# Trainium2 kernel: the stage between two attentions with fp16 part products, its operands split by the attention before it

## The chip, the cores and the metric

One core of one Trainium2 chip. The metric is the device time of one execution in microseconds (us), as the median of several runs. Engines are named as in the profile: PE is TensorE (PEld its weight loads), DVE VectorE, ACT ScalarE, POOL GpSimd, SP SyncE; SPq and the like are their queues of instructions.

## The reference, cut to what matters

Two layers over 2 x 1024 tokens of 512 features. Each layer computes `x = x + s * g` from the normalized `x`, where `s` is an attention and `g` a gate. The end of the first layer and the start of the second, which the change is about:

```python
out = out.transpose(0, 2, 1, 3).reshape(B, S, LATENT)      # 16 heads x 64 = 1024 features
s = out @ w_o.T                                            # output projection, 1024 -> 512
x = x + s * g
xn = _layernorm(x, axis=-1)
q = (xn @ wq.T)                                            # 32 heads x 16
k = (xn @ wk.T); v = (xn @ wv.T)                           # 8 heads x 16
router_logits = jnp.einsum('bsd,hd->bsh', xn, Wr) + br     # gate: 8 experts
low = jnp.einsum('bsd,hrd->bshr', xn, A)                   # low-rank part, 8 x 16
```

The second attention picks chunks of keys by their largest score, so queries and keys are wanted at about fp32's precision.

## The kernel before, in words

The program is a row of phases, each a block in which every engine has its own list of instructions, ordered by hand, and waits on semaphores. Between two blocks the engines meet. The change touches `attend_phase` (first attention), `MiddleWeights` and `middle_phase` (stage between the attentions).

**`attend_phase`** (L1905) goes over 16 pairs of heads, `p` from 0 to 15 (4 groups of keys x 2 sequences x 2 pairs). A pair has 8 key tiles `kt` of 128 keys; with the causal mask tile `kt` has 1024 - 128 kt query columns, in one or two pieces of up to 512. A step `n` is 8 p + kt.
- TensorE (L1997 on) makes the scores of a piece as fp16 part products into one of four PSUM banks (L2012 to L2017), up to four pieces ahead of the step whose values it makes next. A bank is free when ScalarE has taken the piece four back. `values(n)` (L2028) multiplies the values with the exponentials in fp32 into `ps_o`; for tile 0 it waits until ScalarE has copied the former pair's `ps_o`. Behind tile 2, `sums(p - 1)` (L2039) adds up the former pair's exponentials over the keys into `ps_n`.
- ScalarE takes each piece's exponential (L2078) into a ring of four steps, `probs`; a step waits until TensorE and the adder of the step four back (VectorE for tiles 0 to 2, GpSimd for 3 to 7) are done. For slots of tile 3 and 4 it waits until GpSimd has added tile 4. Behind tile 0 it copies the former pair's output, `copy(p - 1)` (L2062).
- VectorE adds tiles 0 to 2 of both heads (`gather`, L2124 to L2129) and puts GpSimd's sum to them (`combine(p - 1)`, L2137). `divide(p - 1)` waits for TensorE's sums, takes the reciprocal of 128x1024 sums (L2145) and multiplies the output with it into `stage` (L2150).
- GpSimd adds tiles 3 to 7 (L2097 to L2102).
- SyncE's list loads the stage's weights at the start, the next group's queries, keys and values behind the end of a pair, and stores `stage` (L1964) of the former pair.

```python
            for p in range(ALL):
                gather(p, 0)
                gather(p, 1)
                if p > 0:
                    combine(p - 1)
                gather(p, 2)
                if p > 0:
                    divide(p - 1)
```

**`middle_phase`** (L2264) goes over four chunks `c` of 512 tokens. TensorE's list: `project(0)`, `project(1)`, then `rest(c)`, `project(c + 2)`, `gates(c)`.
- `project(c)` (L2388): for each of four tiles of 128 tokens eight fp32 products of 128x512; VectorE (`add`, L2533) multiplies with the gate and adds `x`. Two PSUM banks, so the third tile waits until VectorE has taken the first.
- VectorE's `norm(c)` (L2540 to L2548), with a power by GpSimd, gives `xn`.
- `rest(c)`: 16 transpositions (L2398), evicted by ScalarE into `xnT` (L2447); values, low-rank part and gate (L2406, 264 columns), evicted at L2451; queries and keys (L2412), five blocks of four fp32 products of 128x512, evicted at L2463. Then VectorE's softmax of the gate (`route`) and the rotation of queries and keys with their split into three bf16 parts (`rotate`, L2581 to L2593; GpSimd's share L2505, L2507).
- `gates(c)` (L2425): the gate's products, with ScalarE's silu.
VectorE's list per chunk is `add(c + 1)`, `route(c)`, `rotate(c)`, `norm(c + 1)`.

## Time and profile before

| what | us |
|---|---|
| median of 3 runs | 2363.93 (2362.97 to 2368.98) |
| the profiled execution: its time / its span | 2369.5 / 2367.7 |
| TensorE, VectorE, ScalarE, GpSimd busy, share of the span | 87%, 63%, 46%, 33% |
| first attention, first product to last multiply | 1051.5 to 1361.8 |
| wait until the stage between starts | 1361.8 to 1371.3 |
| stage between the attentions | 1371.3 to 1664.1 |
| mean granted clock of TensorE | 0.946 |

The table's stages are read from the timeline. Durations below come from this one execution; they can be set against its own time, and that stands 5.6 us above the median of the runs. In the timeline a row gathers neighbouring instructions of one line; a row's form is that of its longest, and the bracket tells how long the engine sat idle before it and what ended that.

### The profile page before, as it was taken

How to read it: one execution, taken by the hardware profiler on the slowest of the kernel's cores; microseconds unless marked ns; L12 is line 12 of the kernel's file. 1: busy time of each engine (PE TensorE's matmuls, PEld its weight loads, DVE VectorE, ACT ScalarE, POOL GpSimd, SP SyncE). 2: the span in 40 equal slices, each digit the busy share in tenths (PEclk: the TensorE clock that was granted, in tenths of full speed). 3: DMA queues.
4: the chain of work that ended last, by engine and by line, in shares of the span. 5: the costliest groups of instructions: out<-in, count | busy, mean ns of one | idle time of the engine just before them, and what ended most of it. 6: DMA issues, size and time to landing. Idle time of an engine off the chain costs nothing. (4 is left out here: it accounts for less than half of the span.)

```text
span 2367.7 us, 46673 instructions
## 1 busy us (share of the span) xinstructions
PE 2058.6 (87%) x19128; PEld 1009.8 (43%) x19128; DVE 1489.3 (63%) x2992; ACT 1100.8 (46%) x1987; POOL 771.9 (33%) x735
## 2 busy tenths in 40 slices
PE   7999989998647898979999789987588888888878
PEld 3444435555213333445555434443244444443434
DVE  3534354443559999716777725445888888888813
ACT  1212135555324333227777502324277777777760
POOL 0102212222447456504444402223343333433310
PEclk9999999999879899989999989997799999999999
DMA  6120101101412121362222264132936455364424
GB/s 240 36 89 36 67 19 32 32 14 44 140 43 83 54 67 32 107 208 75 90 82 76 76 175 143 58 79 76 216 59 84 69 72 81 58 89 65 59 79 142
DMA packets 149338, 198.03 MB, mean 84 GB/s; under 512 B 57154, under 2 KB 85956, under 8 KB 146564
## 3 DMA queue, kind: packets, MB, share of 16 engines
q1 hardware_dynamic: 147540, 181.41, 30.9%
q10 hardware_dynamic: 1584, 13.63, 1.6%
q8 instruction: 151, 2.47, 0.5%
q14 instruction: 63, 0.52, 0.1%
HBM read 134.69 MB, written 60.29 MB: 82 GB/s over the span
## 5 line engine op out<-in xcount | busy, mean ns | idle before, releaser
L3112 DVE TENSOR_REDUCE f_chunk_max<-f_ps_a 128x64 f32<-128x1024 f32 x320 | 319.7, 1033 | 47.4 <-PE f_ps_a L2856 25.0
L2985 ACT ACTIVATE conv_in<-f_ps_s 128x512 f32<-128x512 f32 x480 | 258.5, 602 | 86.6 <-PE f_ps_s L2887 42.7
L2856 PE MATMUL f_ps_a<-conv_in 128*32 128x512 bf16 (+3 forms) x3072 | 201.0, 340 | 42.1 <-DVE f_chunk_max L3112 25.4
L2078 ACT ACTIVATE d_probs<-d_ps_s,d_shift 128x512 f32<-128x512 f32 (+3 forms) x384 | 196.7, 584 | 82.7 <-PE d_ps_s L2017 72.8
L2887 PE MATMUL f_ps_s<-f_qs,f_ks 128*32 128x512 bf16 x2304 | 208.3, 382 | 23.3 <-ACT f_qs L2976 14.7
L1420 PE MATMUL c_ps_c<-conv_in,c_wT 128*128 128x512 f16 x768 | 186.2, 402 | 18.5 <-DVE c_odd L1721 14.1
L3052 POOL TENSOR_SCALAR f_absent<-f_rest 128x576 f32<-128x576 f32 x32 | 54.4, 1700 | 304.9 <-DVE f_rest L3129 180.7
L2909 PE MATMUL f_ps_o<-conv_in,f_v 128*32 128x512 f32 (+2 forms) x1152 | 125.9, 522 | 28.3 <-ACT conv_in L2985 27.4
L2976 ACT ACTIVATE f_qs<-f_ps_s 32x512 bf16<-32x512 f32 x192 | 112.8, 587 | 75.6 <-PE f_ps_s L2870 73.3
L2028 PE MATMUL d_ps_o<-d_probs,conv_in 128*64 128x512 f32 (+3 forms) x768 | 146.1, 488 | 0.0
L2856 PEld LDWEIGHTS f_ps_a<-conv_in 128*32 128x32 bf16 x3072 | 71.8, 98 | 164.3 <-DVE f_chunk_max L3112 68.6
L2388 PE MATMUL e_ps_s<-e_oT,conv_in 128*128 128x512 f32 x256 | 118.7, 626 | 23.2 <-DVEq L64 17.4
L2012 PE MATMUL d_ps_s<-conv_in 128*64 128x512 f16 (+3 forms) x768 | 126.4, 330 | 8.8 <-POOL d_ones L2086 8.8
L2145 DVE RECIPROCAL d_inverse<-d_ps_n 128x1024 f32<-128x1024 f32 x16 | 104.9, 6558 | 44.2 <-PE d_ps_n L2039 44.2
L1420 PEld LDWEIGHTS c_ps_c<-conv_in,c_wT 128*128 128x128 f16 x768 | 77.2, 103 | 129.9 <-issue 36.8
L2016 PE MATMUL d_ps_s<-conv_in 128*64 128x512 f16 (+3 forms) x384 | 124.8, 329 | 0.0
L2017 PE MATMUL d_ps_s<-conv_in 128*64 128x512 f16 (+3 forms) x384 | 124.7, 329 | 0.0
L300 PE MATMUL a_ps_d<-conv_in,conv_more 128*128 128x512 f32 x256 | 119.2, 621 | 0.0
L2887 PEld LDWEIGHTS f_ps_s<-f_qs,f_ks 128*32 128x32 bf16 x2304 | 59.6, 95 | 106.8 <-ACT conv_in L2985 35.0
L798 POOL TENSOR_TENSOR conv_in<-b_tiles,conv_in 128x1024 f16<-128x1024 f32 x16 | 34.1, 2131 | 186.6 <-ACT conv_more L958 186.6
L2388 PEld LDWEIGHTS e_ps_s<-e_oT,conv_in 128*128 128x128 f32 x256 | 51.0, 201 | 89.8 <-issue 82.4
L1420 PE MATMUL c_ps_c<-conv_more,c_wT 128*128 128x512 f16 x384 | 88.3, 384 | 0.0
(364 smaller groups left out, 4451.5 us busy)
## 6 DMA issues: line engine op xcount, KB each, us to landing
conv_in<-qk SPq DMA_DIRECT2D x96, 128.0 KB, 4.0
f_qs<-qk SPq DMA_DIRECT2D x96, 128.0 KB, 4.8
conv_in<-q_parts SPq DMA_DIRECT2D x8, 1024.0 KB, 5.1
o0T<-d_stage SPq DMA_DIRECT2D x16, 512.0 KB, 3.2
conv_in<-o0T SPq DMA_DIRECT2D x4, 2048.0 KB, 10.6
qk<-e_part SPq DMA_DIRECT2D x12, 640.0 KB, 4.9
f_qs<-qk SPq DMA_DIRECT2D x96, 64.0 KB, 4.7
rows<-in_qc_w ACTq DMA_DIRECT2D x3, 1536.0 KB, 7.0
```

The costliest lines, as they stand in the source:

```text
L1420: last = pe.matmul(ps_c[q % RING][:], wT[i][:, w, k, :], conv_of.of(t, x, k), start=(k == 0 and w == 0 and x == 0), stop=(k == MQ - 1 and ...
L2012: pe.matmul(out[sides[e], lo - low:], k_high[b][:, keys[e]], q[b][:, h, lo:hi], start=True, stop=False)
L2016: pe.matmul(out[sides[0], lo - low:], k_low[b][:, keys[0]], q[b][:, h, lo:hi], start=False, stop=True)
L2017: pe.matmul(out[sides[1], lo - low:], k_low[b][:, keys[1]], q[b][:, h, lo:hi], start=False, stop=True)\
L2028: last = pe.matmul(ps_o[a * HD0:(a + 1) * HD0, lo:hi], v[b][:, kt, :], probs[n % RING][a][:, lo:hi], start=(kt == 0), stop=((kt + 1) * P = ...
L2078: act.activation(probs[n % RING][SCORES[c][1]][:, lo:hi], ps_s[c % BANKS][:, lo - hi + CH:], ACT.Exp, bias=shift[:, 0:1], scale=HD0 ** -0. ...
L2388: last = pe.matmul(ps_s[t % 2][:], o_in[c % 2][:, m, t * P:(t + 1) * P], oT[:, m, :], start=(m == 0), stop=(m == MQ - 1))
L2856: last = pe.matmul(out[side(e), h, 0:w], qa[u][:, 2 * p + h, side(e, qt * P)], ka[u][:, kh * CH:kh * CH + w], start=True, stop=not last_keys)
L2887: last = pe.matmul(out[side(e), :], ks[u][:, side(e, kt * P)], qs[u][version][:, :, at:at + P], start=True, stop=not (masked or part))
L2909: last = pe.matmul(ps_o[2 * HD1 * h:2 * HD1 * (h + 1), lo - half * CH:], v[u][:, kt, :], probs[m % HELD][:, h, lo - half * CH:], start=(kt ...
L2985: act.activation(probs[m % HELD][:, :, at:at + P], bank_of["s", i, n][:].rearrange("p (h n) -> p h n", n=P), ACT.Exp, scale=HD1 ** -0.5).t ...
L3112: dve.tensor_reduce(chunk_max[:, qt - 2, :, at:at + w // CHUNK], src.rearrange("p h (c k) -> p h c k", k=CHUNK), AX.X, ALU.max).then_inc(a ...
```

## The change

- The output of the first attention is no longer stored in fp32 but as two fp16 parts, a high one and the rest. ScalarE makes the high part behind tile 6 of the next pair (`high(p - 1)`), VectorE the rest behind its tile 1 (`low(p - 2)`), and SyncE stores both. Each is scaled; the scale comes from the size of the value weights.
- The weights of the output projection, of queries and keys, and of values, low-rank part and gate are measured in the attention (nine squares with a sum on ScalarE, two sends of the sums to memory and two fetches issued from ScalarE's queue, sums on VectorE, a root on GpSimd), then scaled and split by GpSimd in 15 pieces, two per pair from pair 4 on, stored piece by piece from SyncE's queue and loaded back as fp16 parts at pair 12, in the place of the fp32 weights.
- In the stage between, each fp32 product becomes three fp16 ones (high x high, low x high, high x low). The transposed tile is taken by ScalarE as the high part (`xT_high`) and by VectorE as the rest (`lows`, ahead of `route`); a transposition's bank is free when both have taken it. ScalarE and VectorE undo the scales where they empty PSUM.

```diff
@@ -1960,24 +1989,39 @@
-                sp.wait_ge(o_used, p + 1)
-                sp.dma_start(dram["o0T"][g * (G0 // 2) + i, :, b * S:(b + 1) * S], stage[p % 2][:]).then_inc(stored[p % 2], 16)
+                sp.wait_ge(o_low, p + 1)
+                for n in range(2):
+                    sp.dma_start(dram["o0_parts"][n, g * (G0 // 2) + i, :, b * S:(b + 1) * S], o_parts[p % 2][n][:]).then_inc(stored[p % 2], 16)
...
+            def store_pieces(p):
+                for x in range(SPLIT_EACH * (p - SPLIT_FROM), min(SPLIT_EACH * (p - SPLIT_FROM + 1), len(PIECES))):
+                    _, at, n = PIECES[x]
+                    sp.wait_ge(split, 3 * (x + 1))
+                    sp.dma_start(dram["e_parts"][:, :, at:at + n], w_parts[x % 2][:, :, 0:n]).then_inc(split_stored[x % 2], 16)
...
             for p in range(ALL):
                 g, b, i = where(p)
+                if SPLIT_FROM < p <= LAST_SPLIT + 1:
+                    store_pieces(p - 1)
...
+                if p == LAST_SPLIT + 1:
+                    for i in range(2):
+                        sp.wait_ge(split_stored[i], 16 * ((len(PIECES) + 1 - i) // 2))
+                    weights.load_parts(sp)
@@ -2061,6 +2105,29 @@
+            def measure(i):
+                act.wait_ge(v_w_loaded if i == 0 else weights.raw_loaded, 16 if i == 0 else 48)
...
+                act.activation(spent[:, 0:MEASURES[i].shape[1]], MEASURES[i], ACT.Square, accum_out=summed[:, i:i + 1]).then_inc(measured, 1)
+
+            def send(first, last, i):
+                act.wait_ge(measured, last)
...
+            def fetch(first, last, i):
+                act.wait_ge(size_stored, 16 * (i + 1))
...
+            def high(p):
+                act.wait_ge(scaled, 2)
+                act.wait_ge(o_used, p + 1)
+                if p >= 2:
+                    act.wait_ge(stored[p % 2], 32 * (p // 2))
+                act.activation(o_parts[p % 2][0][:], stage[p % 2][:], ACT.Identity, scale=weights.scale[:, 0:1]).then_inc(o_high, 1)
...
                 if kt == 0 and p > 0:
                     copy(p - 1)
+                if kt == 6 and p > 0:
+                    high(p - 1)
+                if n == 2:
+                    measure(0)
+                    send(0, 1, 0)
+                elif n == 4:
+                    fetch(0, 1, 0)
+                elif QT < n < QT + SIZES:
+                    measure(n - QT)
+                elif n == QT + SIZES:
+                    send(1, SIZES, 1)
+                elif n == QT + SIZES + 2:
+                    fetch(1, SIZES, 1)
             copy(ALL - 1)
+            high(ALL - 1)
...
+            def split_piece(x):
+
+                own, at, n = PIECES[x]
+                to, src = w_parts[x % 2], weights.whole[:, at:at + n]
+                pool.wait_ge(scaled, 4)
+                if x >= 2:
+                    pool.wait_ge(split_stored[x % 2], 16 * (x // 2))
+                pool.tensor_scalar(src, src, weights.scale[:, own:own + 1], None, ALU.mult).then_inc(split, 1)
+                pool.wait_ge(split, 3 * x + 1)
+                pool.tensor_copy(to[:, 0, 0:n], src).then_inc(split, 1)
+                pool.wait_ge(split, 3 * x + 2)
+                pool.tensor_tensor(to[:, 1, 0:n], src, to[:, 0, 0:n], ALU.subtract).then_inc(split, 1)
...
+                elif SPLIT_FROM <= p <= LAST_SPLIT:
+                    for x in range(SPLIT_EACH * (p - SPLIT_FROM), min(SPLIT_EACH * (p - SPLIT_FROM + 1), len(PIECES))):
+                        split_piece(x)
@@ -2146,19 +2251,51 @@
                 if p >= 2:
-                    dve.wait_ge(stored[p % 2], 16 * (p // 2))
+                    dve.wait_ge(o_low, p - 1)
                 dve.tensor_tensor(stage[p % 2][:], o_raw[p % 2][:], inverse[:], ALU.mult).then_inc(o_used, 1)
+
+            def low(p):
+                dve.wait_ge(o_high, p + 1)
+                dve.scalar_tensor_tensor(o_parts[p % 2][1][:], stage[p % 2][:], weights.scale[:, 0:1], o_parts[p % 2][0][:], ALU.mult, ALU.subtract)\
+                   .then_inc(o_low, 1)
...
             for p in range(ALL):
                 gather(p, 0)
                 gather(p, 1)
+                if p > 1:
+                    low(p - 2)
                 if p > 0:
                     combine(p - 1)
                 gather(p, 2)
+                if p == 0:
+                    sizes(0, 1, 0)
+                elif p == 2:
+                    sizes(1, 4, 1)
+                elif p in (1, SPLIT_FROM - 1):
+                    scales(*((0, 1, 0) if p == 1 else (1, 4, 1)))
                 if p > 0:
                     divide(p - 1)
...
@@ -2380,12 +2534,14 @@
-                pe.wait_ge(loaded[c % 2], 144 * (c // 2 + 1))
+                    pe.wait_ge(weights.w_loaded, 32)
...
                 for t in range(TT):
                     pe.wait_ge(s_used, TT * c + t + 1)
                     for m in range(MQ):
-                        last = pe.matmul(ps_s[t % 2][:], o_in[c % 2][:, m, t * P:(t + 1) * P], oT[:, m, :], start=(m == 0), stop=(m == MQ - 1))
+                        for i, (w, x) in enumerate(PARTS):
+                            last = pe.matmul(ps_s[t % 2][:], o_in[c % 2][:, x, m, t * P:(t + 1) * P], oT[w][:, m, :],
+                                             start=(m == i == 0), stop=(m == MQ - 1 and i == len(PARTS) - 1))
                     last.then_inc(s_done, 1)
 
             def rest(c):
...
-                    pe.wait_ge(xnT_ready, KD * c + max(k - 1, 0) + 2)
...
+                        pe.wait_ge(xT_low, KD * c + max(k - 1, 0))
...
-                pe.wait_ge(xnT_ready, KD * (c + 1) + 2)
+                pe.wait_ge(xT_low, KD * (c + 1))
...
-                        last = pe.matmul(ps_y[t % 2][:, 0:TOK], xnT[:, k, t * P:(t + 1) * P], tokT[:, k, :],
...
+                        for i, (w, x) in enumerate(PARTS):
+                            last = pe.matmul(ps_y[t % 2][:, 0:TOK], xT[:, x, k, t * P:(t + 1) * P], tokT[w][:, k, :],
...
-                        last = pe.matmul(ps_q[i % 2][:], qkT[:, i, k, :], xnT[:, k, :], start=(k == 0), stop=(k == KD - 1))
+                        for n, (w, x) in enumerate(PARTS):
+                            last = pe.matmul(ps_q[i % 2][:], qkT[w][:, i, k, :], xT[:, x, k, :],
...
-            primed(act, xnT_ready, 2)
...
-                    act.activation(xnT[:, k, :], ps_t[k % 2][:], ACT.Copy).then_inc(xnT_ready, 1)
+                    act.activation(xT[:, 0, k, :], ps_t[k % 2][:], ACT.Copy).then_inc(xT_high, 1)
...
+                    act.activation(tok[:, t, :], ps_y[t % 2][:, 0:TOK], ACT.Identity, scale=unscale[:, 3:4]).then_inc(tok_ready, 1)
...
+                    act.activation(raw[:, i, :], ps_q[i % 2][:], ACT.Identity, scale=unscale[:, 2:3]).then_inc(raw_ready, 1)
...
-                    dve.tensor_tensor(x1[:, t, :], ps_s[t % 2][:], g_in[c % 2][:, t, :], ALU.mult).then_inc(s_used, 1)
+                    dve.scalar_tensor_tensor(x1[:, t, :], ps_s[t % 2][:], unscale[:, 4:5], g_in[c % 2][:, t, :], ALU.mult, ALU.mult).then_inc(s_used, 1)
...
+            def lows(c):
+                for k in range(KD):
+                    dve.wait_ge(xT_high, KD * c + k + 1)
+                    dve.tensor_tensor(xT[:, 1, k, :], ps_t[k % 2][:], xT[:, 0, k, :], ALU.subtract).then_inc(xT_low, 1)
...
+                lows(c)
...
+            lows(NCH - 1)
...
```

## Rows read from the trace of the kernel before

**Rows 1.** The page: busy time, share of the span, instructions.
```profile
PE 2058.6 (87%) x19128; PEld 1009.8 (43%) x19128; DVE 1489.3 (63%) x2992; ACT 1100.8 (46%) x1987; POOL 771.9 (33%) x735
```

**Rows 2.** Busy time in one pair: PE, PEld, DVE, ACT, POOL, clock, DMA.
```profile
1198.00:1216.37 18.37, 18.37 (x188) 9.72 (x186) 14.34 (x11) 13.09 (x26) 8.20 (x11) 1.00 0.38 129
```

**Rows 3.** Timeline of ScalarE, attention: start, duration, what, idle before.
```profile
1214.83 0.84 ACT L2078 ACTIVATE d_probs<-d_ps_s,d_shift 128x256 f32<-128x256 f32 x2 [0.39 <-PE d_ps_s L2017]
...
1216.13 0.63 ACT L2078 ACTIVATE d_probs<-d_ps_s,d_shift 128x128 f32<-128x128 f32 x2 [0.46 <-PE d_ps_s L2017]
...
1217.43 2.54 ACT L2078 ACTIVATE d_probs<-d_ps_s,d_shift 128x512 f32<-128x512 f32 x4 [0.68 <-POOL d_late L2102]
...
1219.86 1.02 ACT L2062 ACTIVATE d_o_raw<-d_ps_o 128x1024 f32<-128x1024 f32 x1
```

**Rows 4.** Timeline of VectorE, attention.
```profile
1203.60 2.14 DVE L2126 TENSOR_TENSOR d_early<-d_probs 128x896 f32<-128x896 f32 x2 [1.27 <-ACT d_probs L2078]
...
1205.65 1.55 DVE L2137 TENSOR_TENSOR d_early<-d_early,d_late 128x640 f32<-128x640 f32 x2
...
1211.67 6.56 DVE L2145 RECIPROCAL d_inverse<-d_ps_n 128x1024 f32<-128x1024 f32 x1 [2.72 <-PE d_ps_n L2039]
...
1218.26 1.62 DVE L2150 TENSOR_TENSOR d_stage<-d_o_raw,d_inverse 128x1024 f32<-128x1024 f32 x1
```

**Rows 5.** Timeline of TensorE, attention.
```profile
1209.73 1.89 PE L2039 MATMUL d_ps_n<-d_early,d_ones 128*64 128x512 f32 x8
...
1217.57 0.60 PE L2028 MATMUL d_ps_o<-d_probs,conv_in 128*64 128x256 f32 x4
...
1220.93 1.51 PE L2028 MATMUL d_ps_o<-d_probs,conv_in 128*64 128x512 f32 x6
```

**Rows 6.** Timeline of TensorE, stage between the attentions.
```profile
1371.34 58.11 PE L2388 MATMUL e_ps_s<-e_oT,conv_in 128*128 128x512 f32 x128 [17.42 <-DVEq L64]
...
1458.50 13.90 PE L2388 MATMUL e_ps_s<-e_oT,conv_in 128*128 128x512 f32 x32
...
1474.89 15.70 PE L2388 MATMUL e_ps_s<-e_oT,conv_in 128*128 128x512 f32 x32 [2.49 <-DVE e_x L2533]
...
1499.67 7.39 PE L2406 MATMUL e_ps_y<-e_tokT,e_xnT 128*128 128x264 f32 x32 [0.69 <-ACT e_xnT L2447]
...
1506.90 17.33 PE L2412 MATMUL e_ps_q<-e_xnT,e_qkT 128*128 128x512 f32 x40
...
1541.71 17.07 PE L2388 MATMUL e_ps_s<-e_oT,conv_in 128*128 128x512 f32 x32 [3.31 <-DVE e_x L2533]
```

**Rows 7.** Timeline of TensorE, fp16 products of an earlier stage.
```profile
986.92 5.35 PE L1420 MATMUL c_ps_c<-conv_more,c_wT 128*128 128x512 f16 x24
```

**Rows 8.** Timeline of VectorE, stage between: the rotation of chunk 1.
```profile
1514.19 0.72 DVE L2581 STREAM_SHUFFLE e_swapped<-e_raw 128x512 f32<-128x512 f32 x1
...
1520.86 1.75 DVE L2589 TENSOR_TENSOR e_turn<-e_turn,e_part 128x512 f32<-128x512 f32 x1
...
1532.90 0.68 DVE L2589 TENSOR_TENSOR e_turn<-e_turn,e_part 128x512 f32<-128x512 f32 x1
...
1534.89 2.47 DVE L2540 BATCH_NORM_STATS2 e_stats<-e_x 128x6 f32<-128x512 f32 x4
```

**Rows 9.** Windows behind the two stops: columns as in rows 2.
```profile
1478.00:1480.00 2.00, 2.00 (x4) 0.86 (x3) 0.00 (x0) 0.00 (x0) 0.00 (x0) 0.59 0.00 0
...
1544.00:1546.00 2.00, 2.00 (x3) 0.67 (x2) 0.00 (x0) 0.00 (x0) 0.00 (x0) 0.50 0.00 0
```

**Rows 10.** Groups of GpSimd by line and form: count, busy, mean ns.
```profile
L2099 POOL TENSOR_TENSOR d_late<-d_probs 128x512 f32<-128x512 f32 x32 | 40.1, 1273 | 47.3 <-ACT d_probs L2078 47.3
...
L3052 POOL TENSOR_SCALAR f_absent<-f_rest 128x576 f32<-128x576 f32 x32 | 54.4, 1700 | 304.9 <-DVE f_rest L3129 180.7 <-PE f_ps_s L2887 124.2
...
L2097 POOL COPY d_late<-d_probs 128x128 f32<-128x128 f32 x32 | 9.4, 294 | 120.2 <-ACT d_probs L2078 120.2
```

**Rows 11.** The page: a store of the attention, us to landing.
```profile
o0T<-d_stage SPq DMA_DIRECT2D x16, 512.0 KB, 3.2
```

More of the change, by code:

```diff
@@ L1922, in attend_phase @@
         stage = [sb(f"stage{i}", [P, S]) for i in range(2)]
+        o_parts = [[sb(f"o_part{i}{n}", [P, S], FP16) for n in range(2)] for i in range(2)]
+        spent = sb("spent", [P, KD * MiddleWeights.TOK], BF16)
+        summed = sb("summed", [P, SIZES])
+        w_space = sb("w_space", [P, SIZES * P])
+        sized, v_w = w_space, w_space[:, 0:KD * KVD]
+        size = sb("size", [P, 4])
+        root = sb("root", [P, 4])
+        w_parts = [w_space[:].bitcast(FP16)[:, n * 2 * (CH + 16):(n + 1) * 2 * (CH + 16)].rearrange("p (a c) -> p a c", a=2) for n in range(2)]
         temp = sb("temp", [P, 1])
@@ L1945, in attend_phase @@
         stored = [sem(f"d_stored{i}") for i in range(2)]
+        v_w_loaded = sem("d_v_w_loaded")
+        measured = sem("d_measured")
+        size_stored = sem("d_size_stored")
+        size_loaded = sem("d_size_loaded")
+        size_step = sem("d_size_step")
+        rooted = sem("d_rooted")
+        scaled = sem("d_scaled")
+        split = sem("d_split")
+        split_stored = [sem(f"d_split_stored{i}") for i in range(2)]
+        o_high = sem("d_o_high")
+        o_low = sem("d_o_low")
+        lo_w, hi_w = weights.ends[0:3], weights.ends[1:4]
+        MEASURES = [v_w[:]] + [weights.whole[:, at:min(at + 2 * CH, hi)] for lo, hi in list(zip(lo_w, hi_w))[0:2] for at in range(lo, hi, 2 * CH)] \
+            + [weights.whole[:, lo_w[2]:hi_w[2]]]
+        OWN = ((0, 1), (1, 5), (5, 8), (8, 9))
+        PIECES = [(1, at, CH) for at in range(lo_w[0], hi_w[0], CH)] + [(2, at, CH) for at in range(lo_w[1], hi_w[1], CH)] \
+            + [(3, lo_w[2] + i * (CH + 16), CH + 16) for i in range(2)]
+        SPLIT_FROM, SPLIT_EACH = 4, 2
+        LAST_SPLIT = SPLIT_FROM + (len(PIECES) - 1) // SPLIT_EACH
         PAIRS = B * G0 // 2
@@ L1979, in _ @@
             for i in range(2):
-                sp.wait_ge(stored[i], 16 * (ALL // 2))
+                sp.wait_ge(stored[i], 32 * (ALL // 2))
         def halves(kt):
@@ L2169 @@
 class MiddleWeights:
+    TOK = KV1 * HD1 + HL * RL + HL
+    NQK = D // P + KV1 * HD1 // P
+    WIDTHS = MQ * D, NQK * KD * P, KD * TOK
+    COLS = sum(WIDTHS)
     def __init__(self, ctx, nc, dram, sem, space, used):
```

88 lines of the change are left out of this document (67 added, 21 removed).

## The prediction

> **What bounds the kernel now.** I read the page first: TensorE is busy 87% of the span [rows 1], so nearly every other engine's work is cover. Then I split the two stages that the change touches by the timeline, since a share of the whole span says nothing about either.
>
> In the attention the kernel repeats one pair of heads every 18.37 us, 16 times, and in that stretch TensorE is busy 18.37 of 18.37 us at full clock, ScalarE 13.09, VectorE 14.34, GpSimd 8.20 [rows 2]. So TensorE sets the time, and ScalarE has 5 us per pair to give, but only where they lie. Where they lie is the point of this prediction. ScalarE's order in a pair is: eight key tiles' exponentials, with the copy of the former pair's output behind tile 0. The row at 1214.83 is tile 6, ending 1215.67; tile 7 is at 1216.13; the next pair's tile 0 at 1217.43; the copy at 1219.86 [rows 3]. VectorE's order is: add tile 1 (1203.60), combine (1205.65), tile 2, then the reciprocal of the former pair's sums from 1211.67 for 6.56 us, and the multiply with it from 1218.26 for 1.62, so done at 1219.88 [rows 4]. The reciprocal can't be earlier: TensorE makes the sums behind tile 2, 1209.73 to 1211.6, and goes on [rows 5]. **The former pair's output is finished 4.2 us after ScalarE has ended tile 6** (1219.88 against 1215.67). Before the change nobody waits for it there.
>
> In the stage between the attentions TensorE leads the first two chunks (58.11 us without a stop), later TensorE and a chain over ScalarE, VectorE and GpSimd take turns: the second half of a projection waits 2.49 and 3.31 us for VectorE [rows 6]. So there a faster TensorE is paid back only in part.
>
> **The change, part by part. First the gain.** A 128x512 fp32 product takes 13.90/16 = 0.86 us, two instructions [rows 6]; three fp16 ones take 3 x 0.216 = 0.65 (24 in 5.35 us less a tail of 0.17) [rows 7].
> - Projection of chunks 0 and 1, all on the path: 64 x 0.86 = 55 of the 58.1 us, the other 3 being the half clock at its start, which stays. With 0.65: 41.5 + 3. Gain 13.5.
> - Projection of chunks 2 and 3: its first half runs while VectorE still rotates, gain nothing; its second half is on the chain: 13.9 to 10.4, gain 3.5, twice: 7.
> - Values, low-rank part and gate (264 columns): 7.39 us [rows 6] to 48 x 0.11 = 5.3 at the same rate per column, 2 us in each of four chunks: 8.
> - Queries and keys: 17.33 to 13 us, but VectorE's rotation, 1514.19 to 1534.89, hides all but the first of five blocks [rows 6, 8]: 0.8 + 0.5 per chunk: 5.
> - VectorE's new subtraction of the transposed tile, 128x512 to fp16, 0.68 us as an addition of that size with GpSimd idle [rows 8]: from the third tile on each transposition waits for ScalarE and VectorE in turn, two pairs deep, and the last one stands before the products: about 2.2 us, four times: +9. The scaled evictions cost what the plain ones do.
> - The stop before the second half of a projection grows from 2.5 and 3.3 to some 9 us, so the clock falls for both: +1.5.
> Sum for this stage: -13.5 - 7 - 8 - 5 + 9 + 1.5 = **-23**. Were everything counted at TensorE's saving (128 + 80 products x 0.21, and 8), it would be -52; were only the first two chunks faster, -10.
>
> **Then the attention.** ScalarE's queue gets one 128x1024 activation per pair, the fp16 high part, behind tile 6 of the next pair, with a wait for the multiply. Behind it in the same queue stand tile 7 and everything after; TensorE waits for those. High part: from 1219.9, 1.02 us as the copy of that size [rows 3], so tile 7 starts at 1220.95 in place of 1216.13. TensorE can hold four score blocks ahead; it ends tile 6's values at 1218.1 [rows 5] and needs tile 7's first exponential for the next, at 1221.35: it stops 3.2 us. Tile 7 ends 1221.5, tile 0 and the copy follow without their old gaps, 3.45 us as before: 1225.0, where the copy ended 1220.88. Tile 0's values wait for that copy (they started 1220.93 [rows 5]), so the pair moves by **4.1 us, in 15 pairs: +62**. It doesn't heal: the next reciprocal starts from sums that have moved too.
>
> **The clock.** Behind a stop of 2.49 us the second half of a projection took 15.70 us in place of 13.90, behind 3.31 us (17.07) the granted clock was 0.50; the first case shows 0.59 [rows 6, 9]. So a stop like the new one costs 1.8 to 3.2 us in a dense stretch. Here tile 0 is bound by ScalarE, with about 1.2 us of TensorE's time free, so 0.5 to 2 a pair; I take 1.2: **+18**, bounds 0 and 30.
>
> **GpSimd.** It splits 15 pieces of 512 or 528 columns, two per pair, ahead of its own sums, in pairs 4 to 11. Nearest rows: scaling 576 columns 1.70 us, so 1.5; a copy of 128 columns 0.29, so some 0.9 for 512; subtraction as an addition of 512, 1.27 [rows 10]. A piece is 3.7, two are 7.5. A piece's buffer is free when the Sync queue has stored it, and that queue stands first behind VectorE's low part of two pairs back (about 4.6 us before the reciprocal); with 3 to 4 us for a store [rows 11] the split starts about when the reciprocal does, and ends 7.5 later. Then tile 3's copies (0.6) and tile 4's additions (2.5), for which ScalarE's tile 7 waits by the ring of four: 10.7 after the reciprocal's start against 9.3 by the stall. So +1.5 in seven pairs, 10, and pair 4, where splitting falls on VectorE's additions, 3: **+13**. Bounds: 0 and 30, the latter if stores land 2 us later. The Trainium skill (GPSIMD Engine Reference, Engine selection) calls GpSimd's operations with one input roughly line-rate; by that scaling and copy would be estimated at 0.5 us each, two pieces 4.7, and this term only pair 4's 3. The rows give no one-input operation of this size at such a rate, so my sum stays with the rows.
>
> **Setting up the scales.** Nine squares of up to 1056 columns on ScalarE, 1.05 each by the copy's row, one in pair 0 and eight from tile 1 of pair 1: of 9.5 us ScalarE's gaps take half, +5. Two sends and two fetches are issued from its queue, +1. In pair 2 VectorE waits for the fetched sizes ahead of its reciprocal: fetch behind tile 3, landing some 5 us later, three reductions, so 4.6 after the reciprocal could start: +4.6. The send writes single numbers, for which no row stands; if it lands late, ScalarE waits with the fetch. Together **+10**, bounds 3 and 20. VectorE's low part (1.25 to 1.6 by the multiply) fits between tile 1 and the sums: the combine ended at 1207.2, 2.5 us before TensorE began them [rows 4, 5]; that cover is gone only while GpSimd splits at the same time. The pieces' transfers and the reload of the 4 MB of weights lie in the attention at a DMA share of 0.38 [rows 2]: nothing.
>
> **The end of the attention**: high part, low part and a second store stand between the last multiply and the start of the projection: **+2.5**.
>
> **Sum:** -23 + 62 + 18 + 13 + 10 + 2.5 = +82. The profiled execution took 2369.5 us, span 2367.7; with the change 2451. The median of three runs shown is 2363.9, 5.6 below it, so I predict **2445 us**, 3.4% slower.
>
> **Rivals.**
> (a) *The wait is hidden, and it is faster.* Place: ScalarE behind tile 6. It decides at a multiply that ends by 1215.7, or at TensorE having 4.1 us in hand. Then only the smaller terms stay: -23 + 3 + 5 + 2.5 is -12, 2351 us. Against it: 8.2 us of VectorE work lie between sums and product, 4.2 between sums and the end of tile 6, in every pair. For it: only that I could have a pair's number wrong; the copy's place contradicts that. 0.08.
> (b) *The stall alone,* full clock and fast splitting: -23 + 62 + 3 + 7 + 2.5 = +52, 2415 us. For it: 3.2 us is near the edge of the two stops that I know. 0.22.
> (c) *VectorE and GpSimd hold each other up* while splitting. VectorE's 512-column operation takes 1.75 us beside GpSimd's in place of 0.68 [rows 8]. If the pieces fall on VectorE's additions in all eight pairs, the combine comes 3 us late and TensorE stops a second time: +25 to +35, 2475 us. Against it: the Sync queue's order moves the split under the reciprocal. 0.13.
> (d) *Near no change:* the stage between gives TensorE's full 52, and half of the stall is absorbed: 2363 to 2375. 0.04.
> My forecast has 0.53.
>
> **Chances and range.** A measurement of this kernel can tell 0.3%, 7 us, from no change. (a) gives faster 0.08; (d) same 0.03; the rest, a last 0.01 of (d) with it, slower: 0.89. The range takes (b) at its middle and (c) at its middle: 2408 to 2482.
>
> **What would show it.** ScalarE idle some 4 us behind tile 6 in each pair from 1 to 15, put down to VectorE's multiply; pairs 22.5 to 25 us apart; TensorE idle 3 us or more in each, granted clock of a pair well under the 1.00 of now; attention 80 to 120 us longer; the first two projections 44 to 45 us; projection to the next attention 20 to 26 us shorter. Wrong would be: pairs still 18.4 us apart, or GpSimd named as the one for whom ScalarE waits most.

## The result, and the profile after

The changed kernel takes 2438.56 us (median of 4 runs, 2437.09 to 2439.71) against 2363.68 for the kernel before (4 runs beside it, 2362.97 to 2368.98): a ratio of 1.0311, 95% interval 1.0294 to 1.0329. That is 3.1% slower; 2445 with a range of 2408 to 2482 was forecast. The profiled execution has a span of 2437.6 us against 2367.7.

By stages, profile against profile, each from its first product to the first product of the next stage:

| | before | after | difference | forecast |
|---|---|---|---|---|
| from the start to the attention, unchanged code | 1051.5 | 1046.3 | -5.2 | 0 |
| the attention | 319.9 | 416.4 | +96.5 | +105.5 |
| the stage between | 292.7 | 271.5 | -21.2 | -23 |
| from there to the end, unchanged code | 703.6 | 703.4 | -0.2 | 0 |

The first row is no effect of the change: no instruction ahead of the attention was touched, and over the twelve profiled kernels of this document that start lies anywhere from 1043.4 to 1055.0. The profiled execution of the kernel before stood 5.6 us above the median of its runs, which fits the 5.2 us. The other three rows add up to +75.1, and the medians differ by 74.9.

The page, the line that answers to [rows 1]: TensorE has 22 us less to do, and VectorE, ScalarE and GpSimd have more.

```profile
PE 2036.1 (84%) x19400; PEld 995.0 (41%) x19400; DVE 1523.0 (62%) x3033; ACT 1127.0 (46%) x2021; POOL 818.7 (34%) x782
```

**The stop behind tile 6.** The timelines of ScalarE, VectorE and TensorE around one pair's end answer to [rows 3], [rows 4] and [rows 5]. Columns: start, duration, engine, line, operation, and in the bracket the idle time before it.

```profile
1172.42 0.84 ACT L2145 ACTIVATE d_probs<-d_ps_s,d_shift 128x256 f32<-128x256 f32 x2 [0.39 <-PE d_ps_s L2061]
1177.53 1.15 ACT L2129 ACTIVATE d_o_part<-d_stage,e_scale 128x1024 f16<-128x1024 f32 x1 [4.27 <-issue]
1178.59 2.92 ACT L2145 ACTIVATE d_probs<-d_ps_s,d_shift 128x128 f32<-128x128 f32 x6
1181.36 1.05 ACT L2106 ACTIVATE d_o_raw<-d_ps_o 128x1024 f32<-128x1024 f32 x1
```

```profile
1169.26 6.56 DVE L2250 RECIPROCAL d_inverse<-d_ps_n 128x1024 f32<-128x1024 f32 x1 [0.64 <-PE d_ps_n L2083]
1175.85 1.60 DVE L2255 TENSOR_TENSOR d_stage<-d_o_raw,d_inverse 128x1024 f32<-128x1024 f32 x1
```

```profile
1175.16 0.60 PE L2072 MATMUL d_ps_o<-d_probs,conv_in 128*64 128x256 f32 x4
1178.98 0.41 PE L2056 MATMUL d_ps_s<-conv_in 128*64 128x512 f16 x2 [3.22 <-ACT d_probs L2145]
```

ScalarE ends tile 6 and then sits 4.27 us. The bracket says "issue", which names nobody; the cause is read by laying the timelines side by side: the multiply ends at 1175.85 + 1.60 = 1177.45, and the high part starts 0.08 us later. TensorE sits 3.22 us, until tile 7's exponentials have begun. Lines from the list of waits of the attention (us in total, times, longest):

```profile
PE d_ps_s L2056 <- ACT d_probs L2145: 68.0, 17, 7.5
...
POOL e_whole L2178 <- DMA e_parts<-d_w_space: 65.9, 7, 10.7
ACT d_o_part L2129 <- issue: 55.7, 13, 4.9
...
DVE d_size L2267 <- DMA d_w_space<-sizes: 28.2, 2, 18.3
...
ACT d_probs L2145 <- DMA sizes<-d_summed: 17.0, 2, 9.2
...
ACT d_o_part L2129 <- DVE d_stage L2255: 12.4, 2, 9.7
```

The first and the third line are for the most part this stop, seen from TensorE and from ScalarE. In the two pairs (1 and 2) that the third line leaves out, the last line names VectorE's multiply (`d_stage`, L2255) as the one for which the high part waits. The distances of the pairs, from one copy of the output to the next, are in the table of intervals below.

**The scales' setting up.** The fourth and the fifth line belong to it: ScalarE stands twice behind its own small store, and in pair 2 VectorE's reciprocal stands behind the adding up of the fetched sizes. ScalarE's rows and those of its queue, VectorE's rows, and the list of transfers (size, us from issue to landing):

```profile
1103.54 0.41 ACTq L2116 DMA_DIRECT2D sizes<-d_summed  x1
...
1117.29 0.34 ACTq L2121 DMA_DIRECT2D d_w_space<-sizes  x1
1117.75 2.94 ACT L2145 ACTIVATE d_probs<-d_ps_s,d_shift 128x512 f32<-128x512 f32 x6 [7.80 <-DMA sizes<-d_summed]
1130.38 1.15 ACT L2129 ACTIVATE d_o_part<-d_stage,e_scale 128x1024 f16<-128x1024 f32 x1 [9.69 <-DVE d_stage L2255]
```

```profile
1121.22 1.34 DVE L2267 TENSOR_REDUCE d_size<-d_w_space 128x1 f32<-128x512 f32 x3 [9.90 <-DMA d_w_space<-sizes]
1122.48 6.55 DVE L2250 RECIPROCAL d_inverse<-d_ps_n 128x1024 f32<-128x1024 f32 x1
```

```profile
sizes<-d_summed ACTq DMA_DIRECT2D x1, 0.5 KB, 12.6
sizes<-d_summed ACTq DMA_DIRECT2D x1, 4.0 KB, 13.7
```

**The stage between**, timeline of TensorE, against [rows 6]:

```profile
1462.65 44.08 PE L2543 MATMUL e_ps_s<-e_whole,conv_in 128*128 128x512 f16 x192 [16.50 <-DVEq L66]
...
1512.43 7.05 PE L2564 MATMUL e_ps_y<-e_whole,e_xT 128*128 128x264 f16 x48 [1.42 <-DVE e_xT L2714]
1519.32 13.11 PE L2571 MATMUL e_ps_q<-e_xT,e_whole 128*128 128x512 f16 x60
...
1532.70 10.52 PE L2543 MATMUL e_ps_s<-e_whole,conv_in 128*128 128x512 f16 x48
1552.64 12.40 PE L2543 MATMUL e_ps_s<-e_whole,conv_in 128*128 128x512 f16 x48 [9.42 <-DVE e_x L2692]
...
1575.60 5.57 PE L2564 MATMUL e_ps_y<-e_whole,e_xT 128*128 128x264 f16 x48 [1.42 <-DVE e_xT L2714]
```

The first two projections went from 58.11 to 44.08 us. The 264-column products, 7.39 before, take 7.05 in this chunk and 5.57 in the next: the same 48 instructions, at two clocks.

### The profile page after: what moved, and what is told of

Read it like the earlier page. It is cut to its first block and busy times, and to the rows that moved or that the text cites. A ratio compares the mean times of both kernels' runs of the same rounds, so it can differ in the third digit from the quotient of the medians.

```text
span 2437.6 us, 47417 instructions
## 1 busy us (share of the span) xinstructions
PE 2036.1 (84%) x19400; PEld 995.0 (41%) x19400; DVE 1523.0 (62%) x3033; ACT 1127.0 (46%) x2021; POOL 818.7 (34%) x782
## 5 line engine op out<-in xcount | busy, mean ns | idle before, releaser
L3053 PE MATMUL f_ps_s<-f_qs,f_ks 128*32 128x512 bf16 x2304 | 209.3, 384 | 23.2 <-ACT f_qs L3142 14.6
L2056 PE MATMUL d_ps_s<-conv_in 128*64 128x512 f16 (+3 forms) x768 | 137.4, 360 | 76.9 <-ACT d_probs L2145 68.0
L2061 PE MATMUL d_ps_s<-conv_in 128*64 128x512 f16 (+3 forms) x384 | 135.9, 358 | 0.0
L2060 PE MATMUL d_ps_s<-conv_in 128*64 128x512 f16 (+3 forms) x384 | 135.9, 358 | 0.0
L2543 PE MATMUL e_ps_s<-e_whole,conv_in 128*128 128x512 f16 x384 | 89.4, 397 | 36.1 <-DVE e_x L2692 19.6
L2056 PEld LDWEIGHTS d_ps_s<-conv_in 128*64 128x64 f16 x768 | 47.6, 119 | 120.7 <-ACT d_probs L2145 89.4
L1422 PE MATMUL c_ps_c<-conv_more,c_wT 128*128 128x512 f16 x384 | 93.5, 400 | 0.0
```

The costliest lines, as they stand in the source:

```text
L1422: last = pe.matmul(ps_c[q % RING][:], wT[i][:, w, k, :], conv_of.of(t, x, k), start=(k == 0 and w == 0 and x == 0), stop=(k == MQ - 1 and ...
L2056: pe.matmul(out[sides[e], lo - low:], k_high[b][:, keys[e]], q[b][:, h, lo:hi], start=True, stop=False)
L2060: pe.matmul(out[sides[0], lo - low:], k_low[b][:, keys[0]], q[b][:, h, lo:hi], start=False, stop=True)
L2061: pe.matmul(out[sides[1], lo - low:], k_low[b][:, keys[1]], q[b][:, h, lo:hi], start=False, stop=True)\
L3053: last = pe.matmul(out[side(e), :], ks[u][:, side(e, kt * P)], qs[u][version][:, :, at:at + P], start=True, stop=not (masked or part))
```

## The experiments

Times between two copies of a pair's output, read from ScalarE's timeline, in us. The first interval runs from the copy in pair 1 to that in pair 2, so the interval of pair p is the one of number p. Pair 4 is the first that splits weights in the changed kernel, pair 5 in the kernels with later sizes:

| kernel | the 15 intervals |
|---|---|
| before | 18.4 fourteen times, 16.0 |
| changed | 24.0, 33.1, 23.6, 23.2, 23.2, 24.8, 24.6, 24.5, 23.0, 25.1, 23.3, 23.2, 22.6, 22.8, 21.6 |
| high part behind the copy | 20.0, 21.7, 24.8, 20.8, 24.2, 24.9, 23.9, 25.0, 24.1, 26.3, 19.6, 18.8, 18.8, 18.8, 16.4 |
| high part at tile 2 | 20.1, 22.8, 19.5, 18.4, 28.1, 26.7, 27.0, 27.2, 27.2, 27.5, 22.7, 18.4, 18.4, 18.4, 16.0 |
| filled gap | 24.0, 34.6, 22.3, 22.9, 22.9, 23.6, 24.9, 22.9, 22.9, 24.9, 23.3, 22.3, 22.3, 22.3, 20.7 |
| sizes later | 25.2, 23.5, 22.6, 22.8, 23.2, 23.8, 24.0, 25.2, 22.8, 23.4, 23.0, 22.0, 23.2, 22.6, 21.2 |
| pieces stored early | 24.0, 31.0, 23.3, 23.2, 23.1, 22.7, 23.2, 23.2, 23.1, 24.2, 22.5, 23.1, 23.2, 22.6, 21.2 |
| tile 2, sizes later, stores late | 20.9, 19.0, 18.4, 18.4, 18.4, 25.8, 26.2, 26.7, 27.0, 27.2, 27.3, 22.8, 18.4, 18.4, 16.0 |
| the same, stores early | 21.0, 19.0, 18.4 twelve times, 16.0 |
| and pieces apart | 20.1, 19.0, 18.4, 18.4, 18.8, 19.3 five times, 19.4, 18.4, 18.4, 18.4, 16.0 |

The lengths of the stages in the profile of each kernel, read as in the table of the result. No edit of an experiment touches the last column, and it still varies by up to 11 us from one execution to the next. So an effect of a few us is read from the stage that the edit touches, and not from the whole time:

| kernel | attention | stage between | all the rest |
|---|---|---|---|
| before | 319.9 | 292.7 | 1755.1 |
| changed | 416.4 | 271.5 | 1749.7 |
| 1, high part behind the copy | 385.8 | 271.0 | 1753.1 |
| 2, high part at tile 2 | 396.5 | 270.9 | 1747.5 |
| 3, filled gap | 410.1 | 274.6 | 1752.3 |
| 4, sizes later | 396.9 | 274.4 | 1757.7 |
| 5, pieces stored early | 407.6 | 273.8 | 1758.2 |
| 6, all three | 330.3 | 271.5 | 1747.1 |
| 7, and pieces apart | 335.1 | 274.4 | 1752.6 |
| 8, 7 kept busy | 336.4 | 264.6 | 1747.9 |
| 9, 6 kept busy | 329.1 | 262.3 | 1755.2 |
| 10, 6 with late stores | 385.5 | 271.5 | 1755.7 |

**1. High part behind the copy, one pair later.** The multiply is done there, so the wait is gone; nothing else changes within the loop.

```diff
-                if kt == 6 and p > 0:
-                    high(p - 1)
+                if kt == 0 and p > 1:
+                    high(p - 2)
...
             copy(ALL - 1)
+            high(ALL - 2)
             high(ALL - 1)
```

> One edit on the changed kernel: the high part of a pair is made two pairs later, behind the copy at tile 0, when the multiply has just ended, instead of behind tile 6 of the next pair. Theory (ScalarE waits in order for VectorE's multiply, and TensorE stops behind it): the stop goes, pairs fall from 23 to 25 us back to 18.5 to 19.5, the first 15 pairs' delay of some 5.3 us each is gone but for about 0.5 us of the activation itself: 2438.6 - 65 = 2373 us, between 2362 and 2385. Rival (the extra work of ScalarE, VectorE and GpSimd together is what lengthens the pair, wherever the activation stands): pairs stay at 21 us or more, over 2405 us.

Measured: 2411.01 us (4 runs), ratio to before 1.0189 (1.0164 to 1.0215). Faster than the changed kernel by 28, but outside what was expected, and in the range of the rival (over 2405). The intervals say where: 18.8 in the pairs behind the splitting, 21 to 26 in the eight that split. The stall theory holds for the first, and something else takes its place in the second. The rival, that the added work by itself makes a pair longer wherever the activation stands, is answered by experiment 6, where the same work runs in pairs of 18.4.

**2. High part at tile 2, low part behind tile 2's addition.** A milder place for both.

```diff
-                if kt == 6 and p > 0:
-                    high(p - 1)
+                if kt == 2 and p > 1:
+                    high(p - 2)
...
-                if p > 1:
-                    low(p - 2)
                 if p > 0:
                     combine(p - 1)
                 gather(p, 2)
+                if p > 1:
+                    low(p - 2)
...
```

> As the run before it, but the high part stands behind tile 2 of the pair after the next, where ScalarE had a gap of its own, and VectorE's low part behind its addition of tile 2, ahead of the reciprocal. Theory: no stop, and no delay of the values of tile 1 by the activation: 18.4 to 18.7 us a pair, 2360 to 2375 us, equal to the run before or up to 8 us faster. Rival (sum of work): as above, over 2405 us.

Measured: 2422.2 us, 1.0244 (1.0212 to 1.0276): missed by 47. The pairs behind the splitting are at 18.4 as before the change, to the tenth. Of those that split, pairs 5 to 10 are at 27 to 28, but pair 4, whose two buffers are still free, is at 18.4 as well: it isn't the splitting that costs, but the wait for a buffer. This second wait is now legible, in the rows of GpSimd, SyncE's queue and ScalarE in one such pair:

```profile
1198.51 1.56 POOL L2179 TENSOR_SCALAR e_whole<-e_whole,e_scale 128x512 f32<-128x512 f32 x1 [11.90 <-DMA e_parts<-d_w_space]
...
1206.74 2.48 POOL L2205 TENSOR_TENSOR d_late<-d_probs 128x512 f32<-128x512 f32 x2
```

```profile
1194.84 0.81 SPq L1994 DMA_DIRECT2D o_parts<-d_o_part  x2
1195.69 1.20 SPq L2000 DMA_DIRECT2D e_parts<-d_w_space  x2
```

```profile
1209.30 3.17 ACT L2145 ACTIVATE d_probs<-d_ps_s,d_shift 128x128 f32<-128x128 f32 x6 [8.07 <-POOL d_late L2205]
```

The pieces' store stands in SyncE's queue behind the output's store, which waits for VectorE's low part. So it goes at 1195.7; GpSimd, which has waited 11.9 us for its buffers, splits from 1198.5 to 1206.3, adds tile 4 until 1209.2, and at 1209.30 ScalarE may write tile 7. In the changed kernel the same chain ran its course inside the stop of 4.3 us and behind the reciprocal, where the prediction had priced it at 1.5 us a pair. The two delays overlapped: taking one away laid the other bare.

**3. The gap filled.** 28 idle fp16 products of 64 x 512 into the banks of the sums, free again, while TensorE waits behind tile 6.

```diff
+                if n % QT == 6 and n > QT:
+                    b = where(n // QT)[1]
+                    pe.wait_ge(inverse_ready, n // QT)
+                    for _ in range(7):
...
```

> The changed kernel with its stop left as it is, but TensorE fills it in pairs 1 to 15: behind the values of tile 6 it waits for the reciprocal (which has just read the sums' banks) and makes 28 products of 64x512 fp16 into these banks, some 3 us at full clock, whose results nobody reads. If the stop also costs by the half clock behind it (my term: 1.2 us a pair, 18 in all), the granted clock in the attention goes from 0.93 to 0.95 in a pair to about 1.00 and the time falls by 8 to 18 us, to 2420 to 2430. If the half clock costs nothing, since ScalarE sets the pace there, it stays within 3 us of 2438.6, or gets slower by what the filling runs over the end of the wait.

Measured: 2438.61 us, 1.0305 (1.028 to 1.033): no difference in the whole time, where 8 to 18 us were expected. Windows over two pairs, in the changed kernel and then in this one (columns as in rows 2; the clock is the third number from the end):

```profile
1158.00:1181.25 23.25, 20.03 (x194) 10.19 (x190) 17.41 (x11) 13.89 (x27) 14.66 (x16) 0.95 0.31 103
1181.25:1204.50 23.25, 19.18 (x178) 9.63 (x176) 16.18 (x11) 14.23 (x27) 13.68 (x14) 0.93 0.13 46
```

```profile
1158.00:1181.25 23.25, 22.40 (x216) 10.91 (x212) 17.28 (x12) 14.31 (x28) 14.37 (x15) 1.00 0.30 101
1181.25:1204.50 23.25, 22.20 (x214) 11.20 (x216) 16.28 (x11) 14.35 (x28) 14.67 (x16) 1.00 0.18 55
```

The clock did fall behind the stop, and the filling held it at full. It is worth little: the thirteen intervals from the third on sum to 298.3 against 305.5 us, 0.6 each. The attention is 6.3 us shorter in the profile, and what this kernel loses again lies where the edit touches nothing: 3.1 us in the stage between and 2.6 in all the rest. So the whole time can't settle an effect of this size, and the reading rests on one profile of each kernel.

**4. Sizes later.** The two fetches three and five steps further behind their sends, the second group of sizes a pair later, splitting from pair 5 on.

```diff
-        SPLIT_FROM, SPLIT_EACH = 4, 2
+        SPLIT_FROM, SPLIT_EACH = 5, 2
...
-                elif n == 4:
+                elif n == 7:
...
-                elif n == QT + SIZES + 2:
+                elif n == 3 * QT:
...
-                elif p == 2:
+                elif p == 3:
                     sizes(1, 4, 1)
```

> The changed kernel with the stop left, but ScalarE fetches the sizes later (behind tile 7 of pair 0 in place of tile 4, at tile 0 of pair 3 in place of tile 3 of pair 2), VectorE adds them up one pair later and GpSimd splits from pair 5 on. In the trace of the change ScalarE stood 9.24 and 7.80 us for the sums' stores, and VectorE's reciprocal of pair 2 behind the second fetch. If these waits are on the path: 12 to 22 us faster, 2417 to 2427. If TensorE had work in hand or the wait only moved the one for the multiply: under 5 us.

Measured: 2426.93 us, 1.0255 (1.0227 to 1.0283), 11.6 less than the changed kernel, at the edge of what was expected. ScalarE's wait for its own send fell from 17.0 us to one of 4.8. The attention is 19.5 us shorter in the profile, and the parts that the edit doesn't touch were longer in this execution. The term is real; by this profile and the medians it is between 12 and 20 us.

**5. Pieces stored early.** In the pair that makes them, ahead of the output's store.

```diff
-                if SPLIT_FROM < p <= LAST_SPLIT + 1:
-                    store_pieces(p - 1)
+                if SPLIT_FROM <= p <= LAST_SPLIT:
+                    store_pieces(p)
```

> The changed kernel with the stop at tile 6 left, but the Sync queue stores a pair's weight pieces in that pair's own turn, so GpSimd no longer waits for VectorE's low part of two pairs back (65.9 us of waiting in seven pairs) and splits at the start of a pair. Theory: on the path of the changed kernel that wait cost only what ran over the end of the stop, 1.5 to 2.8 us in three pairs; it now goes, but the splitting falls on VectorE's additions, as in pair 4 of the changed kernel (23.2 us long, like its neighbours without splitting): 2430 to 2440 us. Rival (c) of the prediction (the two engines hold each other up and the combine comes late): pairs of 25 us or more, over 2445.

Measured: 2434.47 us, 1.0294 (1.0257 to 1.033), as expected; against the changed kernel's 1.0311 that is within the scatter. The intervals are clearer: the eight that split sum to 185.4 us against 191.7, eight times 23.2, which is what a pair without splitting takes. So the late stores cost the changed kernel some 6 us. GpSimd's wait for the stores, 65.9 us, is gone from the list of waits; ScalarE's for the multiply is still there (55.6). Splitting now falls beside VectorE's additions, which rival (c) had as the case that costs 25 to 35 us more; it cost nothing.

**6. All three together**: the edits of 2, 4 and 5 in one kernel, of which the core is

```diff
+                if kt == 2 and p > 1:
+                    high(p - 2)
...
+                elif n == 3 * QT:
...
+                    store_pieces(p)
```

> Three edits together on the changed kernel: high part behind tile 2 of the pair after the next, sizes fetched later, pieces stored in their own turn. Theory: all three waits are gone from ScalarE; pairs of 18.4 us outside the splitting, 18.5 to 21 in the eight splitting pairs (GpSimd and VectorE share what is left); stage between 271.5 us: 2363.9 - 21 + 2.5 + 8 + up to 20 = 2350 to 2372. If VectorE and GpSimd hold each other up badly (rival c), 24 us in the splitting pairs and over 2385.

Measured: 2354.11 us (10 runs), **0.9949 (0.9931 to 0.9966): 0.5% faster than the kernel before**, and within what was expected. All intervals but the first two are the old 18.4. The stage between is still 271.5 us.

**7. The same, with one of the two pieces split behind tile 3's copies.**

```diff
-                    for x in range(SPLIT_EACH * (p - SPLIT_FROM), min(SPLIT_EACH * (p - SPLIT_FROM + 1), len(PIECES))):
-                        split_piece(x)
+                    split_piece(SPLIT_EACH * (p - SPLIT_FROM))
...
+                    if kt == KT_POOL and SPLIT_FROM <= p <= LAST_SPLIT and SPLIT_EACH * (p - SPLIT_FROM) + 1 < len(PIECES):
+                        split_piece(SPLIT_EACH * (p - SPLIT_FROM) + 1)
```

> As the run before it, but GpSimd splits one piece at the pair's start and the other behind its copies of tile 3, where it had 3 us of waiting. Theory: less of the splitting falls on VectorE's additions, none holds up tile 4's sums by more than 1 us: 2345 to 2362 us, up to 10 us faster than the run before. Rival: no difference of over 3 us, if the order on GpSimd didn't matter.

Measured: 2362.18 us (10 runs), 0.9985 (0.997 to 1.0001), 8 slower than 6 where up to 10 faster was expected. By the profiles 4.8 us of that lie in the attention; 2.9 lie in the stage between, which the edit doesn't touch. The second piece stands ahead of tile 4's addition, and ScalarE's tile 7 waits for that, in ScalarE's row and in GpSimd's:

```profile
1185.28 2.94 ACT L2145 ACTIVATE d_probs<-d_ps_s,d_shift 128x128 f32<-128x128 f32 x6 [2.33 <-POOL d_late L2204]
```

```profile
1178.29 2.52 POOL L2179 TENSOR_SCALAR e_whole<-e_whole,e_scale 128x512 f32<-128x512 f32 x1
1180.88 0.61 POOL L2181 CAST d_w_space<-e_whole 128x512 f16<-128x512 f32 x1
1181.57 1.16 POOL L2183 TENSOR_TENSOR d_w_space<-e_whole,d_w_space 128x512 f16<-128x512 f32 x1
1182.69 2.50 POOL L2204 TENSOR_TENSOR d_late<-d_probs 128x512 f32<-128x512 f32 x2
```

**8 and 9. TensorE kept busy in the stage between.** Seven idle fp16 products ahead of each chunk's 264-column products, forty ahead of the second half of the projections of chunks 2 and 3; 8 is kernel 7 with this, 9 is kernel 6 with it.

```diff
                 for t in range(TT):
+                    if c >= 2 and t == 2:
+                        pe.wait_ge(tok_ready, TT * (c - 1))
+                        for _ in range(40):
+                            pe.matmul(ps_y[0][:], oT[0][:, 0, 0:P], oT[0][:, 0, :], start=True, stop=True)
                     pe.wait_ge(s_used, TT * c + t + 1)
...
+                pe.wait_ge(raw_ready, NQK * c + 2)
+                for _ in range(7):
+                    pe.matmul(ps_q[0][:], oT[0][:, 0, 0:P], oT[0][:, 0, :], start=True, stop=True)
                 pe.wait_ge(xT_low, KD * (c + 1))
```

> As the run before it, and in the stage between TensorE makes 7 idle fp16 products between each chunk's transpositions and the products behind them, and 40 in the 9 to 10 us before the second half of the last two projections, into banks that are free. In the changed kernel the values, low-rank part and gate took 7.05, 5.57, 7.24 and 8.03 us, where 5.4 was full clock, and the second halves 12.40 and 11.87 in place of 10.5. Theory (half clock behind a slack stretch): 5 to 8 us faster than the run before. Rival (the products were not on the path): within 3 us.

> The kernel with all three edits (2354.1 us: high part at tile 2, sizes later, pieces stored in their own pair), with seven idle fp16 products ahead of the 264-column products of each chunk and forty ahead of the second halves of the projections of chunks 2 and 3, as in the kernel kept warm. Theory (half clock behind slack stretches costs 5 to 10 us in the stage between, whatever the attention does): 264-column products at 5.6 us, second halves at 10.5, stage between some 264.5 in place of 271.5: 2345 to 2349 us, 0.6 to 0.8% faster than the kernel before. Rival (the 7.5 us found beside the split pieces came from the stage's state there, which was 3 us slower): within 3 us of 2354.

Measured: 8 has 2354.65 us (10 runs), 0.9959 (0.9938 to 0.998), 7.5 below 7. 9 has **2348.53 us** (6 runs, 2344.83 to 2349.51), 0.9934 (0.9918 to 0.9949), 5.6 below 6. The intervals of 6 and 9 overlap (their ratios are 0.0015 apart, 3.5 us), but the stage itself is plain: from 271.5 to 262.3 us. Of these 9.2 us, 1.1 lie in the first two projections (44.11 to 43.00), ahead of the first idle product; the other 8.1 lie behind it.

```profile
1380.37 43.00 PE L2548 MATMUL e_ps_s<-e_whole,conv_in 128*128 128x512 f16 x192 [19.41 <-DVEq L66]
...
1429.06 5.57 PE L2572 MATMUL e_ps_y<-e_whole,e_xT 128*128 128x264 f16 x48
...
1467.80 10.53 PE L2548 MATMUL e_ps_s<-e_whole,conv_in 128*128 128x512 f16 x48 [0.79 <-DVE e_x L2700]
```

The four 264-column groups take 5.57, 5.57, 5.58, 5.56 here against 7.05, 5.57, 7.24, 8.03 in the changed kernel; the second halves 10.53 twice against 12.40 and 11.87. Together these six groups are 8.8 us shorter.

**10. Kernel 6 with the stores late again**: the direct trial of the second wait.

```diff
-                if SPLIT_FROM <= p <= LAST_SPLIT:
-                    store_pieces(p)
+                if SPLIT_FROM < p <= LAST_SPLIT + 1:
+                    store_pieces(p - 1)
```

> Late sizes and the high part at tile 2 with the low part behind the gather of tile 2, as in the kernel with all three edits (2354.1 us), but the pieces stored one pair later again, behind the store of the output. Theory: the second wait that the stall had covered is this store alone. Then the seven pairs that split are 25 to 28 us apart again (the second experiment had 26.7 to 28.1) against 18.4 with early stores, GpSimd waits some 12 us per pair for the pieces' stores and ScalarE some 8 for GpSimd's sums: 2354 + 7 x 8.5 = 2405 to 2420 us. Rival: the early stores do not matter once the sizes come late, and the pairs stay at 18.4 to 19.5 us: 2354 to 2362 us.

Measured: 2415.88 us, 1.0208 (1.0182 to 1.0235), as expected. Two lines of SyncE's queue are worth 62 us here (55 by the length of the attention) and some 6 in experiment 5. The waits of this kernel:

```profile
POOL e_whole L2179 <- DMA e_parts<-d_w_space: 83.6, 7, 12.4
...
ACT d_probs L2145 <- POOL d_late L2205: 53.4, 8, 8.5
```

## Why the prediction was right, and where its terms were off

**The stall** (+62): right, in place, mechanism and size. ScalarE's idle time behind tile 6 was forecast at 4.2 us and is 4.27, the stop of TensorE at 3.2 and is 3.22. With the gap filled a pair without splitting takes 22.3 us, 3.9 above 18.4, so 59 in 15 pairs. Experiment 2 shows the cause: with the high part elsewhere those pairs are back at 18.4. The rival (a), in which the wait is hidden, is out.

**The clock** (+18): right in kind, too large. The pairs without splitting take 23.2 us for the most part, and with the clock held at full 22.3; over all 13 intervals the difference is 0.6, which gives some 8 us for 15, and with 0.9 throughout it would be 13. The step that failed was to carry what a stop costs in a dense row of products to a stretch where ScalarE sets the pace, and to take the middle of 0.5 to 2. That ScalarE's pace is why it costs so little was not tried apart.

**GpSimd** (+13): some 6, by experiment 5. A piece took 1.56 + 0.61 + 1.16 = 3.3 us and about 3.45 with the gaps, 3.7 was forecast, and the split started at 1190.51 beside a reciprocal that started at 1191.57, as worked out. The Trainium skill (GPSIMD Engine Reference, Engine selection) calls GpSimd's operations with one input roughly line-rate. The cast agrees: 0.61 us for 512 columns, where the prediction had estimated 0.5 from that rule. The scaling does not: 1.56, as the nearest row had it. The forecast had priced this term as what runs over the end of the stall (10.7 against 9.3 us behind the reciprocal's start), and did not ask what the same chain costs without the stall: its rival (a), in which the stall is gone, took 3 us for it. It costs 55 to 62 there (experiment 10). For the forecast that made no difference. For the two remedies it did, and both were missed.

**Setting up the scales** (+10): undersized. Counted from the attention's own first product, the third copy comes 30.0 us late, 9.6 of it two stalled pairs, so 20.4: some 10 in pair 0, where ScalarE stood 9.24 us at the first fetch, and most of the rest in pair 2. The step that failed is "two sends and two fetches, +1": the stores of single numbers land 12.6 and 13.7 us after their issue, and ScalarE stood 17.0 us at the fetches. The text had named this wait without a price. In experiment 4 the same reading gives 6.3 in place of 20.4.

**The end of the attention** (+2.5): from the last multiply to the last store's issue it is 2.6 us more, as forecast. But from the last copy to the stage's first product it is 22.6 us in the changed kernel against 25.2 before, so the term came out at -2.6. This belongs to the stall and not to the two smaller stores: the kernels with the stall left (3, 4, 5) have 22.7 to 23.5, those without it 27.3 to 28.6, with the same two stores.

**The pieces together.** In the attention 20.4 for the setting up, 72 to 73 for the pairs (15 times the 4.8 us by which a pair without splitting is longer, stall and clock in one), 6 for GpSimd and -2.6 for the end give the measured 96.5. The forecast's 105.5 is near it in part by luck: the setting up was forecast 10 us too low, the clock, GpSimd and the end together 17 to 22 too high.

**The stage between** (-23): -21.2, and its parts in part by luck as well. The first two projections gained 14.0 (13.5 forecast). The 264-column products were to gain 8 and gained 1.7 (four times the 7.39 of [rows 6], 29.6, against 7.05 + 5.57 + 7.24 + 8.03 = 27.9), since three of four ran partly at half clock. The second halves went from 15.70 + 17.07 to 12.40 + 11.87, a gain of 8.5 where 7 less 1.5 was forecast. The prediction let the clock cost 1.5 more there behind the longer stops; counted from full clock it cost 5.0 before (two times 13.90) and 3.2 after (two times 10.52), though the stops grew from 2.49 and 3.31 to 9.42 and 10.22 us. VectorE's subtraction cost less than the 9 taken for it: from the start of the transpositions to the products it is 5.9 us a chunk against 4.4. Experiment 9 says what the clock behind the slack stretches was worth in this stage: 8 to 9 us.

**Rivals.** (b), the stall alone at 2415, had no clock term and 3 for GpSimd, where some 8 and 6 were found; it lost by the setting up as well, 7 against 20. (c) did not happen: with splitting on VectorE's additions (pair 4 of the changed kernel, and all splitting pairs of experiments 5 and 6) VectorE's operations stretch, and the pairs stay as they were. (d) is out: the stall was not absorbed, and the stage between gave 21 us and not 52.

Left open: why the clock costs nothing in some pairs and over 1 us in others. Three pairs of the changed kernel show ScalarE waiting for GpSimd behind the high part, 5.9 us in all, which is about the whole of GpSimd's term.

## What to carry to other kernels

An instruction added to an engine with time to spare costs nothing only if its operand is ready when its turn comes: compare the moment at which the operand is finished with the moment at which the instruction in front of it ends, and place it behind the first instruction that satisfies that, a whole iteration later if need be. Behind the copy a pair took 18.8 us, at tile 2 18.4: among the places that satisfy it, one in a gap of the engine is the better. Before a stall is removed, list every other chain that runs in its shadow, the stores that free buffers above all, and look for the one that is late next: here the first of three remedies alone gave 28 or 16 of the 75 us, the second 12, the third 4 (within the scatter), and the three together 84. A store queued behind another that waits for late data is itself late.

## What was not expected of the hardware

- A store of 128 single numbers (0.5 KB) took 12.6 us to land and one of 128 x 8 (4 KB) 13.7, where the halves of the output, 256 KB each, had a median of 2.3 over the kernel. Both small ones ran beside loads that kept the transfer engines full (share 1.00 and more), and the two halves that were issued 4.4 us behind the 4 KB store took 10.1 as well. In kernel 6 those loads ended some 5 us behind the issue of the 4 KB store, and it still took 11.0. How much is the shape and how much the loads was not tried.
- The granted clock of a pair with a stop of 3.2 us was 0.93 to 0.95, and holding it at full gave back 0.6 us a pair. In the stage between, transpositions with stops of 0.5 and 1.4 us around them were followed by products at a clock of 0.62 over 4 us (kernel 6), so for the most part at the lower of the two levels, 1.2 in place of 2.4 GHz, and the 48 products took 7.06 us in place of 5.57. In the next chunk of the same kernel, behind stops of the same length, they ran at 1.00 and took 5.57; what decides between the two wasn't tried. Forty idle products that run while TensorE would only wait brought the second halves from 12.40 and 11.88 to 10.53 each.
- GpSimd's scaling of 128x512 took 1.56 us alone and beside VectorE's reciprocal (changed kernel, 1193.97), and 2.4 to 2.8 beside other operations of VectorE (kernels 6 and 7); its cast to fp16 took 0.61 and 1.2 to 1.5. That brought no loss as long as nobody waited for them.
